# Attention of an adaLN block on eight cores: two heads side by side in the score matmuls

## What is computed

```
h = _layernorm(x, axis=-1) * (1 + ca) + sa
qkv = jnp.einsum('bnd,ed->bne', h, W_qkv)          # 16 heads, Dh = 64
scores = jnp.einsum('bhnd,bhmd->bhnm', q, kk) * scale
A = jax.nn.softmax(scores, axis=-1)
out = jnp.einsum('bhnm,bhmd->bhnd', A, v)
x = x + ga * out
...
wq = jnp.clip(jnp.round(w * scale), -1.0, 1.0) / scale   # ternary weights of the FFN
```

## Time and profile before

| | |
|---|---|
| time, median of two runs | 3730.47 us (3717.29 to 3743.66) |
| the profiled execution's own time | 3721.69 us |
| its span on the slowest core | 3720.2 us (the others 3701.7 to 3719.6) |
| PE busy | 2736.7 us (74%) |
| DVE busy | 1655.6 us (45%) |
| ACT busy | 1107.3 us (30%) |
| mean granted TensorE clock | 0.705 of full speed |
| attention, first L735 to first L881 | 619.6 to 2297.1 us |

### The profile page before, as it was taken

The page is one execution under the profiler, slowest core; times in us unless marked ns, Lnnn a source line. Parts: engine busy times, 40 slices in busy tenths (PEclk is TensorE's granted clock), DMA queues, the critical chain, the costliest instruction groups (busy, mean ns, idle before and its releaser), DMA issues.

```text
span 3720.2 us, 29998 instructions; the slowest of 8 cores (3701.7 to 3720.2 us)
## 1 busy us (share of the span) xinstructions
PE 2736.7 (74%) x8156; PEld 754.7 (20%) x8156; DVE 1655.6 (45%) x2454; ACT 1107.3 (30%) x1199; POOL 243.6 (7%) x445
## 2 busy tenths in 40 slices
PE   6526754999999999999999997121856856856866
PEld 1102320111111111111111111010312312322322
DVE  0275563434244333434244334667463563464464
ACT  0100025324333333323333332234341341242232
POOL 0000000101111011101111110000000000000000
PEclk9858965676666666676666666555967967977977
DMA  6439821212112112212122113322404414414413
GB/s 211 158 118 252 233 92 32 51 28 59 42 51 51 35 42 52 51 29 59 40 52 51 37 41 129 129 79 91 130 32 150 130 37 144 125 48 134 129 54 111
DMA packets 209158, 327.38 MB, mean 88 GB/s; under 512 B 135985, under 2 KB 136242, under 8 KB 194658
## 3 DMA queue, kind: packets, MB, share of 16 engines
q1 hardware_dynamic: 167122, 226.88, 19.4%
q0 software_dynamic: 41872, 98.59, 10.2%
HBM read 289.68 MB, written 42.01 MB: 89 GB/s over the span
## 4 chain that ended last, share of the span: by engine, by line
PE 52%; DVE 24%; DMA 10%; ACT 8%; issue 5%; DVEq 1%; SPq 0%; ACTq 0%; POOL 0%; POOLq 0%
PE sps L742 13%; PE sps L735 13%; PE avps L779 5%; PE dops L783 5%; PE dps L1396 3%; DVE gq L1328 3%; PE avps L775 2%; DVE vq L1355 2%; DVE gpb L1232 2%; DVE gup L1245 2%; DVE mab L1258 2%; DMA wc<-wqkvT 2%; ACT sgb L1240 2%; PE bcps L801 2%; ACT sgb L1250 2%
## 5 line engine op out<-in xcount | busy, mean ns | idle before, releaser
L751 ACT ACTIVATE PT<-sps 128x1024 bf16<-128x1024 f32 x512 | 524.3, 1024 | 515.0 <-PE sps L742 514.8
L808 DVE RECIPROCAL bcsb<-bcps 128x512 bf16<-128x512 f32 x64 | 214.9, 3358 | 946.9 <-PE bcps L801 926.5
L742 PE MATMUL sps<-Qc,Kc 64*128 64x512 bf16 x1024 | 523.0, 612 | 0.0
L735 PE MATMUL sps<-c,onesb 1*128 1x512 bf16 x1024 | 511.0, 599 | 9.3 <-DMA c<-C8h 8.7
L1218 PE MATMUL gps<-hA,tg 128*128 128x512 bf16 x1024 | 250.3, 388 | 189.8 <-DMA tu<-ternu 125.1
L779 PE MATMUL avps<-PT,Vc 128*64 128x512 bf16 x512 | 237.8, 465 | 22.8 <-ACT PT L751 22.8
L1341 PE MATMUL dps<-gq,td 128*128 128x512 bf16 x256 | 129.3, 608 | 161.3 <-DVE gq L1328 161.3
L1222 PE MATMUL ups<-hA,tu 128*128 128x512 bf16 x1024 | 245.8, 384 | 0.0
L783 PE MATMUL dops<-PT,onecb 128*1 128x512 bf16 x512 | 219.0, 428 | 0.0
L1240 ACT ACTIVATE sgb<-gpb 128x512 f32<-128x512 f32 x128 | 80.6, 629 | 442.6 <-DVE gpb L1232 442.6
L1396 PE MATMUL dps<-gq,td 128*128 128x512 bf16 x768 | 174.1, 389 | 30.9 <-DMA td<-ternd 30.8
(11 more groups left out here) (171 smaller groups left out, 2625.1 us busy)
## 6 DMA issues: line engine op xcount, KB each, us to landing
tg<-terng SPq DMA_DIRECT2D x128, 256.0 KB, 2.8
tu<-ternu SPq DMA_DIRECT2D x128, 256.0 KB, 3.1
td<-ternd POOLq DMA_DIRECT2D x32, 1024.0 KB, 6.4
wmb<-wmod SPq DMA_DIRECT2D x8, 2048.0 KB, 8.6
xs<-xT SPq DMA_DIRECT2D x16, 1024.0 KB, 6.0
mb<-wgT SPq DMA_DIRECT2D x8, 2048.0 KB, 11.2
mb<-wuT SPq DMA_DIRECT2D x8, 2048.0 KB, 10.4
mb<-wdT SPq DMA_DIRECT2D x8, 2048.0 KB, 9.1
```

Of the source, the lines that this page charges most:

```text
L735: p.inc(TE.matmul(sps[sp][:, n2 * 512:(n2 + 1) * 512], onesb[0:1, :], cb[0:1, cs:cs + 512], start=True, stop=False), eT)
L742: p.inc(TE.matmul(sps[sp][:, n2 * 512:(n2 + 1) * 512], lhsT, Qc[bp:bp + 64, q0:q0 + 512], start=False, stop=True, tile_position=(bp, 0)), eT)
L751: p.inc(S.activation(PT[hb][:, kt * 1024:(kt + 1) * 1024], sps[sp], AF.Exp, scale=0.125), eS)
L808: p.inc(V.reciprocal(bcsb, bcps[:]), eV)
```

## The change

The loop over heads becomes a loop over pairs of heads `c`. In one `kt` PE computes the scores of both heads of the pair. The PSUM for scores is the same four banks, but now split into four buffers of one bank, one for each (par, n2), where n2 is the half of the 1024 queries. The bound is held in two rows, on partition 0 for the even head and on partition 64 for the odd one, and its matmul has a `tile_position` too. There are four exponentials of 512 columns per `kt` where there was one of 1024 per head. `PT[0]` and `PT[1]` hold the two heads in place of the two halves. AV follows for both heads: even, odd, even, odd. The ternary pieces are emitted in kt 1 to 15 (15 per unit of pair and half) and nine more after AV.

```
-        sps = [s0t[:], s1t_[:]]
+        sps = {(0, 0): se0[:], (0, 1): se1[:], (1, 0): so0[:], (1, 1): so1[:]}
...
-        c8row_tok = {(0, 0): p.dma(Y, "Y", "dc80", c80, C8h[0:1, 0:1024])}
-        for h in range(NH):
...
+        p.dma(Y, "Y", "dc80", c8pair[0:1, :], C8h[0:1, 0:1024])
+        c8row_tok = {(0, 0): p.dma(Y, "Y", "dc80", c8pair[64:65, :],
+                                   C8h[1:2, 0:1024])}
+        for c in range(NH // 2):
             for half in range(2):
...
                 for kt in range(NTC):
-                    sp = kt % 2
-                    p.wait(TE, "T", eS, exp_sbuf_tok[sp])
...
                     for n2 in range(2):
-                        p.inc(TE.matmul(sps[sp][:, n2 * 512:(n2 + 1) * 512],
-                                        onesb[0:1, :], cb[0:1, cs:cs + 512],
-                                        start=True, stop=False), eT)
+                        for par in range(2):
+                            p.wait(TE, "T", eS, exp_sbuf_tok[(par, n2)])
+                            if kt == 0 and n2 == 0:
+                                p.wait(TE, "T", "dc80", tok_c8row)
+                            bp = 64 * par
+                            p.inc(TE.matmul(sps[(par, n2)],
+                                            onesb[bp:bp + 1, :],
+                                            c8pair[bp:bp + 1,
+                                                   n2 * 512:(n2 + 1) * 512],
+                                            start=True, stop=False,
+                                            tile_position=(bp, 0)), eT)
...
                     for n2 in range(2):
                         q0 = c * T + half * 1024 + n2 * 512
+                        for par in range(2):
+                            bp = 64 * par
+                            p.inc(TE.matmul(sps[(par, n2)], lhsTs[par],
+                                            Qc[bp:bp + 64, q0:q0 + 512],
+                                            start=False, stop=True,
+                                            tile_position=(bp, 0)), eT)
+                        tok_sc2 = p.cnt[eT]
+                        for par in range(2):
+                            p.wait(S, "S", eT, tok_sc2)
+                            if kt == 0 and n2 == 0:
+                                p.wait(S, "S", eT, pt_avdone[par])
+                            p.wait(S, "S", eS)
+                            p.inc(S.activation(
+                                PT[par][:, kt * 1024 + n2 * 512:
+                                        kt * 1024 + (n2 + 1) * 512],
+                                sps[(par, n2)], AF.Exp, scale=0.125), eS)
+                            exp_sbuf_tok[(par, n2)] = p.cnt[eS]
-                    if 2 <= kt <= 13:
+                    if 1 <= kt <= 15:
                         emit_tern_piece()
...
-                for gg in range(2):
+                for gi, (par, gg) in enumerate([(0, 0), (1, 0), (0, 1), (1, 1)]):
                     gq = half * 2 + gg
-                    avb = gg
+                    avb = gi % 2
...
                     av_evac_tok[avb] = p.cnt[eV]
+                emit_tern_n(9)
```

More of the change, by code:

```diff
@@ L622, in _build_nc_inner @@
     g_bcsb, bcsb = alloc("bcsb", [128, 512], BF16, "right")
-    g_c80, c80 = alloc("c80", [1, 1024], BF16, "right")
+    g_c80, c8pair = alloc("c8pair", [128, 1024], BF16, "right")
     g_tw0, tw0 = alloc("tw0", [128, 256], F32, "right")
@@ L693, in _build_nc_inner @@
     PT = [PT0, PT1]
-    with (nc.psum_tensor("sps0", [128, 1024], F32) as s0t,
-          nc.psum_tensor("sps1", [128, 1024], F32) as s1t_,
+    with (nc.psum_tensor("spsE0", [128, 512], F32) as se0,
+          nc.psum_tensor("spsE1", [128, 512], F32) as se1,
+          nc.psum_tensor("spsO0", [128, 512], F32) as so0,
+          nc.psum_tensor("spsO1", [128, 512], F32) as so1,
           nc.psum_tensor("avps0", [128, 512], F32) as av0t,
@@ L704, in _build_nc_inner @@
         bcps = bct[:]
-        exp_sbuf_tok = [0, 0]
+        exp_sbuf_tok = {(0, 0): 0, (0, 1): 0, (1, 0): 0, (1, 1): 0}
         pt_avdone = [0, 0]
@@ L715, in _build_nc_inner @@
         p.wait(TE, "T", eS, tok_qk_s)
-        c8tok = {}
         p.wait(Y, "Y", "dc8", tok_c8)
-        c8row_tok = {(0, 0): p.dma(Y, "Y", "dc80", c80, C8h[0:1, 0:1024])}
-        for h in range(NH):
[L720 to L723, removed]
+        p.dma(Y, "Y", "dc80", c8pair[0:1, :], C8h[0:1, 0:1024])
+        c8row_tok = {(0, 0): p.dma(Y, "Y", "dc80", c8pair[64:65, :],
+                                   C8h[1:2, 0:1024])}
+        for c in range(NH // 2):
             for half in range(2):
-                hb = half
-                tok_c8row = c8row_tok[(h, half)]
+                tok_c8row = c8row_tok[(c, half)]
                 for kt in range(NTC):
-                    sp = kt % 2
-                    p.wait(TE, "T", eS, exp_sbuf_tok[sp])
-                    if kt == 0:
-                        p.wait(TE, "T", "dc80", tok_c8row)
-                    lhsT = Kc[bp:bp + 64, c * T + kt * 128: c * T + (kt + 1) * 128]
-                    for n2 in range(2):
-                        cs = n2 * 512
-                        p.inc(TE.matmul(sps[sp][:, n2 * 512:(n2 + 1) * 512],
-                                        onesb[0:1, :], cb[0:1, cs:cs + 512],
-                                        start=True, stop=False), eT)
+                    lhsTs = {0: Kc[0:64, c * T + kt * 128: c * T + (kt + 1) * 128],
+                             1: Kc[64:128, c * T + kt * 128: c * T + (kt + 1) * 128]}
+                    for n2 in range(2):
+                        for par in range(2):
[9 more added lines that the diff above has]
+                                            tile_position=(bp, 0)), eT)
                     if kt == NTC - 1:
@@ L756, in _build_nc_inner @@
+                    if 1 <= kt <= 15:
                         emit_tern_piece()
                 tok_exp_all = p.cnt[eS]
-                nh, nhalf = (h, 1) if half == 0 else (h + 1, 0)
-                if nh < NH:
+                nc_, nhalf = (c, 1) if half == 0 else (c + 1, 0)
+                if nc_ < NH // 2:
                     p.wait(Y, "Y", eT, tok_lastr1)
-                    c8row_tok[(nh, nhalf)] = p.dma(
-                        Y, "Y", "dc80", c80,
-                        C8h[nh:nh + 1, nhalf * 1024:(nhalf + 1) * 1024])
@@ L764, in _build_nc_inner @@
-                for gg in range(2):
+                    p.dma(Y, "Y", "dc80", c8pair[0:1, :],
+                          C8h[2 * nc_:2 * nc_ + 1,
+                              nhalf * 1024:(nhalf + 1) * 1024])
+                    c8row_tok[(nc_, nhalf)] = p.dma(
+                        Y, "Y", "dc80", c8pair[64:65, :],
+                        C8h[2 * nc_ + 1:2 * nc_ + 2,
+                            nhalf * 1024:(nhalf + 1) * 1024])
+                for gi, (par, gg) in enumerate([(0, 0), (1, 0), (0, 1), (1, 1)]):
@@ L771, in _build_nc_inner @@
                     for kt in range(NTC):
-                        rhs = PT[hb][:, kt * 1024 + gg * 512: kt * 1024 + (gg + 1) * 512]
+                        rhs = PT[par][:, kt * 1024 + gg * 512:
+                                      kt * 1024 + (gg + 1) * 512]
                         base = kt * 1040 + c * 130
@@ L786, in _build_nc_inner @@
                     if gg == 1:
-                        pt_avdone[hb] = tok_av
-                    if half == 1 and gg == 1:
-                        c8tok[h] = p.cnt[eT]
+                        pt_avdone[par] = tok_av
                     p.wait(S, "S", eT, tok_av)
```

## The result

| | before | changed |
|---|---|---|
| median | 3730.05 us (10 runs) | 3801.59 us (11 runs) |
| ratio | | 1.0196, 95% interval 1.0174 to 1.0217 |
| profiled execution's span, slowest core | 3720.2 us | 3794.2 us |
| spans of the eight cores | 3701.7 to 3720.2 us | 3745.8 to 3794.2 us |
| mean granted TensorE clock by core | 0.703 to 0.707 | 0.698 to 0.706 |

The changed kernel is 2.0% slower. I forecast 3783 us, +1.6% on the profiled execution, and a range that holds the result.

A forecast was written before the change was run, and what follows sets the result against it. PE bounds the scores before, at 3.85 us per kt for two heads; after, ACT and the handshake take turns. Scores 16 x 3.2 = +51, AV 0, edge +10: +61 on 3721.69 gives 3783 us, range 3735 to 3830 (8 in 10: 3735 to 3900).

The forecast's parts named there:

- the chain: Score step: four exponentials, 2.66 us, then a serial gap of 1.46 us through K=1 and K=64 matmuls.
- handover to PE: Score gap: from an exponential's end to the K=1 matmul that waited for it, 0.14 us.
- K=1 to K=64: Score gap: from the K=1 matmul that waited to the first K=64 matmul, 0.53 us.
- K=64 to the exponential: Score gap: from the start of the second K=64 matmul to the exponential, 0.79 us.
- Side by side: Score gap: the two heads' K=64 matmuls run concurrently, adding 0 us rather than 0.40 per step.
- the two obstacles of the nearest rows: Score matmuls before: neighbours either changed shape (0.56 us apart) or shared their partitions (0.40 us apart).
- The rival with 3898 us: Scores: K=64 matmuls run one after the other, gap 1.86 us, +10.4 us per unit, +4.7%; chance 0.30.
- The stretches: Per unit: scores 66.5 us against 63.3 before, +3.2; AV (attention times V) unchanged from 40.8.
- one entry from the low clock less: AV: saves 2 to 3 us per unit, set against an added restart; net 0, with -3 to +2.
- The edge: After the attention: the last nine ternary pieces and a store delay the first update of x, +10 us once.
- The rival of the clock: Scores: granted clock rises from 0.51 to 1.00, -3.8 us per unit, AV -2.5, 3631 us (-2.4%); chance 0.07.

The follow-up runs named there:

- exp512_only: Kernel before with each exponential of 1024 columns cut into two of 512, both after the whole step's matmuls: 3754.82 us, ratio 1.0091 to the kernel before.
- interleave: Changed kernel with PE's order by query half: K=1 and K=64 matmuls of the first 512 queries, then of the second: 3459.61 us, 0.9305 of the kernel before.
- pair_apart: Changed kernel with the even head's K=64 matmuls before the odd head's, first-half exponentials waiting for the third: 3898.56 us, ratio 1.0494 to the kernel before.
- own_wait: Changed kernel with matmuls and exponentials ordered even, even, odd, odd, each exponential waiting for its own K=64 matmul: 3782.35 us, ratio 1.0156 to the kernel before.

## Why the prediction was right, and where it was off

**The bound that moves.** No link of the chain failed. Forecast and trace for one step: exponential 0.60 and 0.597; between two 0.09 and 0.09; handover to PE 0.14 and 0.14; K=1 to K=64 0.53 and 0.51; K=64 to the exponential 0.79 and 0.79. The sum was 4.12 and is 4.11.

**Side by side.** No row of before showed it, and I took the lower bound because none of the two obstacles of the nearest rows was there. The K=64 pairs start 3 to 4 ns apart. The Trainium skill, "TensorE: Matmul & The Clock Gate", Part 3, has some 4 ns for it, and the trace agrees. The rival with 3898 us falls in every trace.

**The stretches.** I forecast 66.5 and 40.8, in sum 107.3 a unit; measured are 66.99 and 40.34, in sum 107.33. The two small errors come for the most part from one thing. The odd head's K=1 matmuls start while bcps still runs on PE:

```profile
1594.27 0.66 PE L811 MATMUL bcps<-drow,onecf 1*128 1x512 f32 x1 [0.99 <-ACT drow L806]
...
1594.40 0.60 PE L734 MATMUL spsO<-c8pair,onesb 1*128 1x512 bf16 x2
1594.78 0.59 PE L811 MATMUL bcps<-drow,onecf 1*128 1x512 f32 x1
```

L734 of spsO is there at 1594.40, ahead of the second row of bcps at 1594.78; that of spsE, which is first in the program, starts at 1595.20. So the scores seem to begin early and AV to end early, by 0.80 us on the mean of the fifteen turns from AV to scores on all cores, and the even head's K=1 still waits. Counted from the even head's K=1, the scores would be 66.2 and AV 41.1. So AV itself hardly moved, as forecast: one entry from the low clock less (4.3 us of low clock per unit in place of 8.5 on the mean of the cores), and more low clock within (7.2 in place of 3.7). I had guessed that these cancel, and they did. That was luck: exp512_only shows that this was no safe guess, since the same part can move by 1.5 us a unit on its own.

**The edge: the mis-sized term.** I had +10 us; it is +16 on the mean and on the slowest core. Nine pieces took 12.7 us and not 10.1 (2357.85 to 2370.58), because DVE twice waited 1.3 to 1.6 us for a load; and the last store and its release took 6.4 us (the idle time ahead of L892) where I had 2.5. In my terms, the loads' waits were taken as nothing, and the store was priced too low. A store of this kind lands in 2.3 us by the median of the page's DMA issues; why the last one took longer is open. I had priced the pieces at the pace they have under the scores, and here DVE waits for their loads and their last store, with nothing to hide either.

**The slowest core.** By the medians the change costs 72 us; I had 61. The edge is 6 of the difference. Where the rest lies can be read from the two traces. The slowest core was core 3 before and is core 6 now, and their spans differ by 74 us: +3 ahead of the attention, +60 in it up to the last multiply (1674.7 to 1735.2), +16 at the edge, -6 behind it. On the mean of the cores the attention grew by 50, as forecast (16 x 3.2 = 51). Core 6 has 10 more, because its AV takes 41.40 us a unit where the mean is 40.76 (here up to the last multiply), with 13.2 us of low clock in a unit where the mean is 11.8: the low clock's share again. The spans of the cores lie 48 us apart, where they lay 18 apart before. Between core 1, the fastest, and core 6 AV makes 22 of the 48 and the work ahead of the attention 18. I had taken one core's rows for all eight and left this out. It is read from one execution of each kernel; no run shows that the wider spread belongs to the change.

**The rival of the clock.** It never rose: 0.51 in every score stretch, in interleave too, where PE is busy for 38 of 40 us. It had a chance of 0.07, and no row speaks for it.

## What to carry to other kernels

Count how many turns of a produce-and-consume chain a loop makes, and what one turn carries. A buffer split more finely is no double buffer: what counts is whether the producer's first instruction for the new round stands behind one that waits for the last consumer of the old round. In this kernel the cure cost no memory and no instruction, only another order, and brought 8.7% of the changed kernel's time. And price work at a stage's end by what it takes alone, not by its rhythm under other work.

## What the runs showed of the hardware

- TensorE started a matmul for partitions 64 to 127 ahead of an earlier one for partitions 0 to 63, 7 ns after the first of them (pair_apart, own_wait), and in the changed kernel a K=1 matmul on partition 64 (1594.40) ahead of the second row of an earlier one on partition 0 (bcps, 1594.78). The semaphore's count still went in program order: 0.76, 1.18, 1.22 and 1.25 us from the first start for the counts one to four. In these runs a wait on a count thus was a wait for all of TensorE's instructions up to it. The Trainium skill, "TensorE: Matmul & The Clock Gate", Part 3 (the mechanism), says that matmuls both start and end in program order; these runs agree for the end as a semaphore shows it, and not for the start.
- Each increment that an exponential waits for beyond the first of a round costs 0.034 to 0.036 us by the medians (0.76 to 0.79, 1.18 to 1.22 to 1.25).
- A K=64 matmul did not start beside a K=1 matmul, also where the two were on different partitions: 0.51 us from the K=1 of the odd half to the K=64 of the even half (1300.35 to 1300.86), 0.56 in the earlier trace rows. In no trace are two such neighbours closer than 0.45 us at the low clock, where pairs of one shape on different halves are 3 to 7 ns apart.
- Stretches of AV with the same instructions took 12.8 or 15.8 us, by the granted clock (0.87 or 0.70). In exp512_only that made 24 of 3755 us without a change in those instructions.
- The granted clock has the two levels 0.5 and 1.0 in the traces before and after, but not in all: in interleave's profiled execution cores 0 and 1 have some 120 us at 0.81 between 1566 and 1913 us, and their AV takes 42.0 and 42.1 us a unit, where the other six have 40.5 to 41.0.
